# Attention scores from two rounded 4-byte parts in row halves, with one ring of three buffers

## The reference, cut to what matters

```
q, k, v = heads(x @ Wq + bq), heads(x @ Wk + bk), heads(x @ Wv + bv)
q, k = rope(q), rope(k)
att = softmax(where(causal, q k^T / sqrt(8), -1e10))
y = att @ v;   x = x + layernorm(y @ Wp + bp)
```

## Time and profile before

| | |
|---|---|
| Median of 3 runs | 1123.39 us (1121.81 to 1124.06) |
| The profiled execution | 1124.22 us, its span 1122.3 us |
| Busy | PE 1048.8 us (93%), DVE 835.8 (74%), POOL 826.6 (74%), ACT 745.5 (66%) |
| Score matmuls, busy over the whole run | L1525 229.8 us, L1566 170.8 us, L1564 168.3 us |
| Word `v`, busy | L1535 174.3 us |
| First word `s` / last | 84.2 us / 808.3 us from the span's start |

### The profile page before, as it was taken

How to read it: one execution, slowest core, us unless ns; L and a number is a source line. 1 busy time by engine, 2 the same in 40 slices (tenths; PEclk the granted TensorE clock), 3 DMA queues, 4 the chain that set the end, 5 groups by cost and what they waited for, 6 DMA issues and landing times.

```text
span 1122.3 us, 26491 instructions
## 1 busy us (share of the span) xinstructions
PE 1048.8 (93%) x8228; PEld 668.9 (60%) x8228; DVE 835.8 (74%) x2265; ACT 745.5 (66%) x1619; POOL 826.6 (74%) x976
## 2 busy tenths in 40 slices
PE   3379999999999999999999999999977999999996
PEld 2255555656666566565665656656453787877742
DVE  5378888888788878888888887887255777777644
ACT  5117778787787877778777787787823666666434
POOL 6536678788888978888788886666844766666757
PEclk8559999999999999999999999999988999999998
DMA  6333333414243242432424323241556444554376
GB/s 95 110 105 119 93 94 113 116 63 121 87 139 113 63 120 73 148 109 74 122 64 140 111 79 112 73 127 38 133 156 106 137 136 137 154 155 134 109 250 199
DMA packets 109747, 129.88 MB, mean 116 GB/s; under 512 B 17723, under 2 KB 90412, under 8 KB 105004
## 3 DMA queue, kind: packets, MB, share of 16 engines
q1 hardware_dynamic: 100908, 110.04, 35.0%
q0 software_dynamic: 8704, 18.17, 4.8%
HBM read 80.99 MB, written 45.50 MB: 113 GB/s over the span
## 4 chain that ended last, share of the span: by engine, by line
PE 77%; DVE 9%; issue 2%; POOL 1%; DMA 1%; ACT 1%; SPq 0%; POOLq 0%; DVEq 0%; ACTq 0%
PE heads_ps L1535 13%; PE score L1525 10%; PE wide L1677 8%; DVE mx L1324 7%; PE wide L1499 6%; PE wide L1564 6%; PE score L1511 4%; PE wide L1566 4%; PE wide L1660 3%; PE wide L1661 3%; PE score L1651 3%; PE wide L1598 2%; PE misc L1543 2%; PE wide L1590 1%; PE wide L1618 1%
## 5 line engine op out<-in xcount | busy, mean ns | idle before, releaser
L978 ACT ACTIVATE values<-score 128x512 f32<-128x512 f32 (+1 forms) x704 | 369.0, 558 | 90.7 <-PE score L1525 81.0
L1324 DVE TENSOR_REDUCE mx<-wide 128x2 f32<-128x1024 f32 (+3 forms) x384 | 387.5, 1039 | 48.5 <-PE wide L1566 45.6
L1525 PE MATMUL score<-qk 75*128 75x512 bf16 (+3 forms) x1024 | 229.8, 301 | 1.7 <-ACT values L978 0.9
L890 POOL TENSOR_SCALAR_AFFINE_SELECT values<-values 128x512 f32<-128x512 f32 x256 | 162.1, 644 | 88.2 <-ACT values L978 87.9
L935 POOL DMA_INDIRECT token_scratch<-spread,e_id x144 | 137.9, 957 | 71.0 <-issue 52.9
L1564 PE MATMUL wide<-qk 72*128 72x384 bf16 (+2 forms) x768 | 168.3, 279 | 9.9 <-DVE mx L1324 4.9
L1535 PE MATMUL heads_ps<-values 128*32 128x512 f32 (+3 forms) x2048 | 174.3, 441 | 0.2 <-POOL values L890 0.2
L1566 PE MATMUL wide<-qk 118*128 118x128 bf16 x1024 | 170.8, 222 | 2.4 <-DVE mx L1324 1.5
L879 POOL DMA_INDIRECT sorted_scratch<-zr,places x128 | 134.0, 1047 | 48.9 <-issue 27.4
L1525 PEld LDWEIGHTS score<-qk 75*128 75x128 bf16 x1024 | 84.8, 98 | 89.8 <-ACT values L978 46.8
L1564 PEld LDWEIGHTS wide<-qk 72*128 72x128 bf16 x768 | 76.0, 99 | 65.5 <-DVE mx L1324 19.0
(11 more groups left out here) (192 smaller groups left out, 1991.3 us busy)
## 6 DMA issues: line engine op xcount, KB each, us to landing
qk<-parts_scratch SPq DMA_DIRECT2D x192, 192.0 KB
parts_scratch<-spread SPq DMA_DIRECT2D x16, 768.0 KB, 8.3
qk<-sorted_scratch SPq DMA_DIRECT2D x144, 66.5 KB
front<-token_scratch SPq DMA_DIRECT2D x16, 512.0 KB, 4.8
xt<-attn_x SPq DMA_DIRECT2D x16, 256.0 KB, 8.6
xr<-attn_x SPq DMA_DIRECT2D x16, 256.0 KB, 8.8
x_scratch<-z SPq DMA_DIRECT2D x16, 256.0 KB, 6.2
shared_scratch<-s_out SPq DMA_DIRECT2D x16, 256.0 KB, 8.8
```

Of the source, the lines that this page charges most:

```text
L890: nc.gpsimd.affine_select(out=prob[n][:, :, 0:P], in_=prob[n][:, :, 0:P], compare_op=ALU.is_ge, fill=0.0, base=0, pattern=[[0, HG], [1, P] ...
L978: nc.scalar.activation(free_ap(prob[kb][:, hs_[0], :], [[1, N * len(hs_)]]), score[SCORE_RING.buffer(b, step)][:, 0:N * len(hs_)], ACT.Exp ...
L1324: nc.vector.tensor_reduce(mx[:, h0:h0 + len(hs_), j:j + 1], src, axis=AX.X, op=ALU.max).then_inc(p1_max, 1)
L1525: last = nc.tensor.matmul(score[SCORE_RING.buffer(b, step)][:, k * N:(k + 1) * N], k4[e][0:SROWS, h, kb * P:(kb + 1) * P], q4[e][0:SROWS, ...
```

## The change

It splits q and k into two parts in a rounded 4-byte format (float32r) in place of three bf16 ones: 4 part products x 8 channels = 32 rows, with the maxima 34, with the stairs 60. Two heads lie one above the other, one in rows 0 to 63 of the array and one in rows 64 to 127, and the two matmuls of a pair follow each other, each into its own bank of a double buffer. The words `second`, `third`, `O` and the stairs' copies go; ACT's part of `N` goes. A step of `s` now covers both banks, six steps for four heads in place of eleven. All of V, X, Q, Y, W, T, p, rX, rL, U, s, D and rows share one ring of three double buffers. Two groups of four heads accumulate into the same output of `v`, in columns 0 to 8 and 9 to 17 of each tile, so the copy, `heads` and the division run for two groups at once. The words that stay keep their order. The stairs are filled by eight transfers from ACT's queue at the start. Cut to its core:

```diff
...
+QPART = 2
+ROWS = QPART * QPART * HS
+SROWS = ROWS + QPART
+STAIR = 5
 MROWS = SROWS + -(-P // STAIR)
 HALF_ROWS = 64
-AHEAD, APART = 2.0 ** 34, 2.0 ** 46
+AHEAD, APART = 2.0 ** 20, 2.0 ** 26
...
+P1_UNITS = [(3, (0,)), (3, (1,)), (2, (0,)), (2, (1,)), (1, (0, 1)), (0, (0, 1))]
+P2_UNITS = [(0, (0,)), (0, (1,)), (1, (0,)), (1, (1,)), (2, (0, 1)), (3, (0, 1))]
+P2_LAST = (1, 3, 4, 5)
...
+NSET = NG // PAIR
...
+    "v3.1@-1 mask2.1 s0.0 p18@0 p19@0 s0.1 v3.2@-1 v3.3@-1 p20@0 s0.2 rnormal heads1@-1 p21@0 mask2.2 s0.3 p22@0 K "
+    "p23@0 s0.4 place s0.5 cos Y v0.0 M1@0 s1.0 N1@0 p0 W mask2.3 rstd s1.1 v0.1 H2 v0.2 v0.3 zstats p1 normal "
+    "mask3.0 U1 G1 s1.2 p2 v1.0 p3 d3 s1.3 mask3.1 p4 mask3.2 d4 s1.4 p5 mask3.3 d5 s1.5 p6 s2.0 p7 v1.1 s2.1 p8 v1.2 "
+    "v1.3 sin0@4 p9 d6 d7 s2.2 U2 H0@-1 sin1@4 mask0.0@1 rstats mask0.1@1 G2 p10 sin2@4 heads0 s2.3 mask0.2@1 "
+    "mask0.3@1 stats d0@-1 V s2.4 s2.5 p11 d1@-1 T v2.0 mask1.0@1 p12 s3.0 d2@-1 M0 zrstd@0 v2.1 N0 p13 sin3@4 Z@0 "
+    "s3.1 rX v2.2 v2.3 mask1.1@1 residual@0 p14 choose s3.2 rL p15 s3.3 chosen rexp X@4 v3.0 mask1.2@1 mask1.3@1 R@4 "
+    "s3.4 U0@-1 G0@-1 p16 s3.5 mask2.0@1 D H1@-1 rrstd@0 Q@4 p17 "
...
+WIDE_STEPS = ("V", "X", "Q", "Y", "W", "T", "p", "rX", "rL", "U", "s", "D", "rows")
...
+    WIDE_RING = Ring(B, lambda step: int(step.what in WIDE_STEPS), 3)
...
-        score = [ctx.enter_context(nc.psum_tensor(f"score{n}", [P, 512], F32)) for n in range(2)]
+        scores_ps = ctx.enter_context(nc.psum_tensor("scores_ps", [P, 2, 512], F32))
+        score = [scores_ps[:, n, :] for n in range(2)]
+        pairs = [*wide, scores_ps]
...
+        parts = view(spread, F32, [2, QPART, T])
+        parts_r = view(spread, F32R, [2, QPART, T])
...
+        qk4 = sb("qk4", [P, 4, NH // 2, T])
+        words = qkr[:].bitcast(F32)
+        q_r = [qkr[:, 2 * n, :, :] for n in range(2)]
+        k_r = [qkr[:, 2 * n + 1, :, :] for n in range(2)]
...
+                heads_ = slice(half * NH // 4, (half + 1) * NH // 4)
+                for side in range(2):
+                    for r in range(QPART):
+                        sp.dma_start(words[rows_of(side, ROWS + r, 1), 2 * e, heads_, :],
+                                     mparts[half][side * NT * NH // 4:(side + 1) * NT * NH // 4, r, :]).then_inc(m_in[half], 16)
...
+                for side in range(2):
+                    at = side * NH // 2 * T + half * run
+                    for a in range(QPART):
+                        q_a, k_all = parts_d[e][0, a], parts_d[e][1, 0]
+                        rows = rows_of(side, a * QPART * HS, QPART * HS)
+                        sp.dma_start(words[rows, 2 * e, heads_, :],
+                                     bass.AP(q_a.tensor, q_a.offset + at, [[NH * T, HS], [0, QPART], [1, run]])).then_inc(shuffled[e][half], 16)
+                        sp.dma_start(words[rows, 2 * e + 1, heads_, :],
+                                     bass.AP(k_all.tensor, k_all.offset + at, [[NH * T, HS], [P * T, QPART], [1, run]])
+                                     ).then_inc(shuffled[e][half], 16)
+                    sp.dma_start(words[rows_of(side, ROWS, QPART), 2 * e, heads_, :],
+                                 free_ap(zero_row[:], [[0, NH // 4 * NT], [1, P]])).then_inc(shuffled[e][half], 16)
...
+                        sp.wait_ge(rows_filled, N_ROWS)
...
-                    sp.wait_ge(part3_ready, 2 * (i + 4))
+                    sp.wait_ge(part2_ready, i + 4)
...
-                    elif step.what == "third":
-                        pool.wait_ge(part2_ready, b + 1)
-                        nc.gpsimd.tensor_tensor(parts[:, n, 2, :], rest[:, n, :], parts[:, n, 1, :],
-                                                ALU.subtract).then_inc(part3_ready, 1)
...
+            for n in range(2):
+                nc.scalar.activation(qkr[0:HALF_ROWS, n, 0, :], free_ap(stairs[:, n, :], [[0, NT], [1, P]]), ACT.Copy).then_inc(stairs_set, 1)
+            act.wait_ge(stairs_set, 2)
+            for e in range(2):
+                for side in range(2):
+                    first = 0 if e or side else 1
+                    for n in range(2):
+                        act.dma_start(words[side * HALF_ROWS + ROWS:(side + 1) * HALF_ROWS, 2 * e + n, first:NH // 2, :],
+                                      free_ap(words[ROWS:HALF_ROWS, n, 0, :], [[0, NH // 2 - first], [1, T]])).then_inc(rows_filled, 16)
...
+                        unit = pairs[WIDE_RING.buffer(b, step)]
...
+                        nc.scalar.activation(free_ap(prob[kb][:, of_[0], :], [[2 * N, 2], [1, N * len(of_)]]),
+                                             free_ap(unit[:, 0, :], [[512, 2], [1, N * len(of_)]]),
                                              ACT.Exp, scale=SCALE).then_inc(exp_done, 1)
...
-                    elif step.what == "v" and n == NT - 1:
+                    elif step.what == "v" and n == NT - 1 and g % PAIR == PAIR - 1:
...
-                    elif step.what == "N":
-                        act.wait_ge(m_rest[n], b + 1)
-                        nc.scalar.activation(mparts[n][:, 1, :], misc[0:NH // 2 * NT, P:2 * P], ACT.Copy).then_inc(m_second[n], 1)
...
+                        for k in range(PAIR):
+                            last = nc.scalar.activation(
+                                free_ap(vext[e][:, 0, 0, :], [[4 * 32, NT * NH // 4], [32, 2], [1, HS]], k * (2 * 32 + WIDTH)),
+                                free_ap(unit[:, 0, :], [[4 * HS, NT * NH // 4], [HS, 2], [1, HS]], k * 2 * HS), ACT.Copy)
...
-                        act.wait_ge(rest_ready, b + 1)
-                        nc.scalar.activation(parts[:, :, 1, :], rest[:], ACT.Copy).then_inc(part2_ready, 1)
+                        nc.scalar.activation(parts_r[:, :, 0, :], unit[:], ACT.Copy).then_inc(part1_ready, 1)
...
+                nc.vector.reciprocal(rinv[:], free_ap(misc[:], [[32, NT * HG], [WIDTH, PAIR]], HS)).then_inc(rinv_ready, 1)
+                dve.wait_ge(rinv_ready, i * NSET + g + 1)
+                for k in range(PAIR):
+                    last = nc.vector.tensor_tensor(free_ap(y[:, 0, :], [[P, NT], [NH // 2 * HS, 2], [HS, 2], [1, HS]], (g * PAIR + k) * 2 * HS),
+                                                   free_ap(misc[:], [[P, NT], [64, 2], [32, 2], [1, HS]], k * WIDTH),
+                                                   free_ap(rinv[:, 0, :], [[HG * PAIR, NT], [2 * PAIR, 2], [PAIR, 2], [0, HS]], k),
+                                                   ALU.mult)
...
-                        nc.vector.tensor_tensor(rest[:], unit[:], parts[:, :, 0, :], ALU.subtract).then_inc(rest_ready, 1)
+                        nc.vector.tensor_tensor(parts_r[:, :, 1, :], unit[:], parts[:, :, 0, :], ALU.subtract).then_inc(part2_ready, 1)
...
+                        nc.vector.tensor_reduce(free_ap(mx[:, c // 4 * 8 + c % 4, j:j + 1], [[NH // 4 * NT, 2], [NT, len(of_)]]),
+                                                free_ap(unit[:, 0, :], [[512, 2], [L, len(of_)], [1, L]]), axis=AX.X,
...
-                    elif step.what == "O":
-                        dve.wait_ge(m_second[n], b + 1)
-                        nc.vector.tensor_tensor(mparts[n][:, 2, :], misc[0:NH // 2 * NT, P:2 * P], mparts[n][:, 1, :],
-                                                ALU.subtract).then_inc(m_ready[n], 1)
+                        nc.vector.scalar_tensor_tensor(out=mparts_r[n][:, 1, :], in0=misc[0:NH // 2 * NT, 0:P], scalar=-1.0,
+                                                       in1=mparts[n][:, 0, :], op0=ALU.mult, op1=ALU.subtract).then_inc(m_ready[n], 1)
...
+                        for k, c in enumerate(2 * g + m for m in of_):
+                            for side in range(2):
+                                rows = slice(side * HALF_ROWS, side * HALF_ROWS + SROWS)
+                                last = nc.tensor.matmul(unit[:, side, k * N:(k + 1) * N], k_r[e][rows, c, kb * P:(kb + 1) * P],
+                                                        q_r[e][rows, c, kb * P:T], start=True, stop=True)
...
+                                                    vext[e][:, n, h4 // 2 * (NH // 2) + 2 * g + h4 % 2, :], prob[n][:, h4, :],
+                                                    start=(g % PAIR == 0 and n == 0), stop=(g % PAIR == PAIR - 1 and n == NT - 1))
...
+                        for k, c in enumerate(n // len(P1_UNITS) * 2 + m for m in of_):
                             if j:
-                                nc.tensor.matmul(o[:, 0:j * P], q4[e][0:ROWS, h, j * P:L], k4[e][0:ROWS, h, 0:j * P],
-                                                 start=True, stop=True)
-                            last = nc.tensor.matmul(o[:, j * P:L], q4[e][0:MROWS, h, j * P:L], k4[e][0:MROWS, h, j * P:L],
-                                                    start=True, stop=True)
+                                for side in range(2):
+                                    rows = slice(side * HALF_ROWS, side * HALF_ROWS + SROWS)
```

(23 more changed lines are left out.)

201 lines of the change are left out of this document (65 added, 136 removed), and 20 rows, old and new, of tables (DRAIN, ORDER, START).

## The result

The changed kernel takes 1249.08 us (median of 4 runs, 1243.54 to 1250.19), the kernel before 1123.62 in the same comparison: a ratio of 1.1113, 95% interval 1.1082 to 1.1144. It is 11% slower where 1061 us were forecast.

The account below looks back on a forecast made before the run. TensorE's matmul columns were taken to bound the kernel; stretches of 42.9 us plus 0.7 for the ring gave 43.6 a turn against 47.5. Savings of 58.5, 1 and 3 us from 1124.2 gave 1061 us, range 1045 to 1095.

Parts of the forecast that it names:

- The pair: Scores: two row halves side by side, each pair costing the larger of its columns and 0.10 us; 10.8 for 17.1 us.
- The loss to VectorE: In S1 and S3, 2.7 us a turn of what TensorE saves is lost because VectorE is late next.
- Where the array changes its shape: Edges of score words: 42 changes a turn at 0.09 us, without waiting for results; nothing added to the sum.
- Rival A: Each of the 42 shape changes waits for results, 0.08 to 0.17 us: 45.7 to 48.4 a turn, 1092 to 1133; chance 0.10.
- The ring: Shared ring of three: words wait for late readers at four places, 0.17 us each, 0.7 a turn; bounds 0 and 3.
- Heads: Two of four heads words go, in S3 and another stretch, saving TensorE 0.45 us each per turn.
- S1: Stretch of the turn from word p18 to p22, where VectorE's maxima set the pace; forecast at 6.0 us.
- The start: Before the loop: shorter parts chain against loading the stairs; 3 us gained, bounds 8 lost to 6 gained.
- the profile's signs: Timeline marks expected if right: pair starts within 0.06 us, turn 43 to 44, VectorE near 88%, p0 near 50.
- S3: Stretch of the turn from word p2 to p9, VectorE nearly full; forecast at 7.5 us, set by VectorE.
- C: Rival for all score words: halves not side by side, 21.6 us for 17.1; 1184 us; chance 0.15 with its worse form.

Follow-up runs that it names:

- keep: Changed kernel plus three unused matmuls of 512 columns a turn, one before s1.4 and two before s1.5: 1237.50 us, 1.1029 of the kernel before.
- max32: Changed kernel with each row maximum taken over only the first 32 columns of its row: 1145.27 us, 1.0169 of the kernel before.
- max32_filled: As max32_split, but each of the 16 added matmuls a turn passes 512 columns in place of one: 1252.37 us, 1.1137 of the kernel before.
- max32_split: max32 plus a one-column whole-array matmul ahead of 16 words s a turn, 32 more shape changes: 1275.80 us, 1.1333 of the kernel before.
- before_max32: The kernel before the change, with each row maximum taken over 32 columns only: 1113.04 us, 0.9903 of the kernel before.
- whole: Changed kernel with every score matmul reading all 128 rows, so no row halves (result changes): 1225.60 us, 1.0912 of the kernel before.

## Why the prediction was wrong

**The pair** was right: side by side in streams and in loads, one clock a column, 0.17 us for two times 384 columns. So were the sizes of the score streams and of ScalarE's exponentials (1024, 811 and 602 ns for the three sizes, 21.2 us a turn for 21.1). The loss to VectorE was right in size: 2.7 us were put down, and keep's turn at 1.00 less max32's is 50.2 - 47.8 = 2.4 (keep's added 0.64 us cost next to nothing: its turns with the dip last 54.6, as the changed kernel's do).

**The step that failed first is "Where the array changes its shape".** It read 0.09 us from the entry of `v` into column tiles, took the 42 changes into and out of row halves for as cheap, and put nothing into the sum for them. A run of row halves costs 0.22 us by the turn, 0.21 by max32_filled and 0.28 by the spacings of max32_split, some 4.7 us a turn for 21 runs. The weight loads (PEld) show what the 0.09 left out; rows of TensorE's timelines, of the kernel before and then of the changed kernel:

```profile
508.13 0.16 PEld L1535 LDWEIGHTS heads_ps<-values 128*32 128x32 f32 x8 [0.43 <-issue]
...
579.92 0.33 PE L1525 MATMUL score<-qk 75*128 75x384 bf16 x1
579.92 0.19 PEld L1579 LDWEIGHTS wide<-gw_sb,hT 128*128 128x128 f32 x1
```

```profile
452.89 0.19 PEld L1566 LDWEIGHTS scores_ps<-gw_sb,hT 128*128 128x128 f32 x1 [0.19 <-issue]
```

Without a change of shape the 4-byte load of gw_sb begins together with the matmul ahead of it, at 579.92. Behind a pair in row halves the same load begins at 452.89, 0.31 us after the pair (452.58) and 0.15 after the pair's columns. The 0.09 of `v` ends where its first load begins (508.13), so the load itself was never in it. Rival A priced each change of shape, 2.1 to 4.8 us a turn, and was given 0.10; its reason, a wait for the results, is not what the starts in max32_split show.

**The second is a step that was not taken:** every duration was read at a granted clock of 1.00, and nothing was priced for its fall. It costs 4.4 us in a turn (keep). It comes with the change: from the first Y to the last every turn of the kernel before holds 1.00, and none of the changed kernel does. The page of the kernel before showed at its start that the clock can fall, and a rival could have been priced from there:

```profile
PEclk8559999999999999999999999999988999999998
```

**The ring** was put at 0.7 us, bounds 0 to 3: with VectorE free the waits that are left are 2.3 in max32 and 0.02 in before_max32. Not all of them need be the ring's; the term was too small, its bounds held.

For a turn: 43.6 + 4.7 for the shape + 0.4 for `heads` + 4.4 for the clock + (2.3 - 0.7) for the waits = 54.7, against 54.6 measured. That this closes is no test of its own, as the terms are differences between these same turns; only the 2.7 for VectorE, in the 43.6, was not taken from them.

**Heads** failed as a term by itself: 0.45 each was TensorE's time of the word, and the work named as hidden ("V's second copy costs ACT some 0.2, hidden in its 11 spare us") is what T waits for. The spare time of ScalarE was elsewhere in the turn. The second multiplication, 0.29 on VectorE in S1, was in the sum.

**The start** was forecast at 3 us gained and lost 10; the bound of 8 lost was too near. The bytes of the stairs were weighed against the first layout, but not against the load of x that they hold up. The first turn, with its clock at 0.67, loses 17.3 us more where 3.9 were to be gained.

Of the profile's signs: pairs within 0.06 held, 1024-column exponentials held, and TensorE waits for maxima in S1 and S3; the turn of 43 to 44, VectorE near 88% (72%: 39.55 of 54.6) and p0 near 50 did not. Of the rivals none had the clock, and the result lies above the dearest form of A (1133) and above C (1184), whose mechanism did not occur.

Not settled: what exactly TensorE's clock answers to. The runs show that it fell with few waits (max32_split) and stayed up where more columns passed (whole, and part of max32_filled); they do not separate columns, rows and shape. Nor was leaving row halves measured apart from entering them over a whole turn.
